# Cross attention and feed-forward on one core: scale sums on ScalarE, bias on the heads, one rope product, rounding by conversion

## What is computed

```python
x = x + xattn(layernorm(x), ctx, ctx, Wq, bq, Wk, bk, Wv, bv, Wo, bo)
x = x + ffn(layernorm(x), w_gate, w_up, w_down)

def xattn(Q, K, V, Wq, bq, Wk, bk, Wv, bv, Wo, bo):      # H = 16, HD = 32
    q, k = rope(heads(Q @ Wq.T + bq)), rope(heads(K @ Wk.T + bk))
    v = heads(V @ Wv.T + bv)
    scores = where(causal, q @ k.T / sqrt(HD), -inf)
    return merge(softmax(scores) @ v) @ Wo.T + bo

def ffn(x, w_gate, w_up, w_down):     # lpbq: blocks of 32, rounded to steps of max/7, clipped to -8..7
    up, gate = qdq(qdq(x) @ lpbq(w_up).T), qdq(qdq(x) @ lpbq(w_gate).T)
    gate = qdq(gate * u16(sigmoid(gate)))
    return qdq(gate * up) @ lpbq(w_down).T
```

## Time and profile before

| | us |
|---|---|
| three timed runs: median (lowest, highest) | 1614.03 (1614.02, 1615.21) |
| the profiled execution: its time | 1613.66 |
| the profiled execution: its span | 1611.8 |
| TensorE busy | 1394.6 (87%) |
| VectorE busy | 1235.3 (77%) |
| ScalarE busy | 921.6 (57%) |
| GpSimd busy | 321.2 (20%) |

### The profile page before, as it was taken

The page is one execution under the profiler, slowest core; times in us unless marked ns, Lnnn a source line. Parts: engine busy times, 40 slices in busy tenths (PEclk is TensorE's granted clock), DMA queues, the critical chain, the costliest instruction groups (busy, mean ns, idle before and its releaser), DMA issues.

```text
span 1611.8 us, 24568 instructions
## 1 busy us (share of the span) xinstructions
PE 1394.6 (87%) x9268; PEld 788.2 (49%) x9268; DVE 1235.3 (77%) x2002; ACT 921.6 (57%) x1994; POOL 321.2 (20%) x326
## 2 busy tenths in 40 slices
PE   4679999999999999967999998999999103999999
PEld 3356666666666667643444444444444001444444
DVE  6657788889898988756888776788899889745641
ACT  2557777777777778755222222899844796321210
POOL 1124444444444444540111110000000000000000
PEclk9879999999999999988999999999999555999999
DMA  5101111111122121111233333577655894534532
GB/s 202 66 8 64 50 65 62 60 65 63 65 79 80 66 80 53 41 42 64 97 113 118 118 112 119 184 250 250 228 183 176 320 356 166 203 137 158 193 132 79
DMA packets 84982, 200.05 MB, mean 124 GB/s; under 512 B 8065, under 2 KB 8065, under 8 KB 84865
## 3 DMA queue, kind: packets, MB, share of 16 engines
q1 hardware_dynamic: 84864, 198.48, 35.2%
HBM read 128.19 MB, written 70.25 MB: 123 GB/s over the span
## 4 chain that ended last, share of the span: by engine, by line
PE 47%; issue 6%; DVE 2%; ACT 0%; POOLq 0%; POOL 0%
PE ffn_banks L1092 31%; PE ffn_banks L1110 16%; PE ffn_banks L1068 1%; DVE ffn_wide L1251 0%; DVE ffn_peaks L1258 0%; DVE ffn_rises L1256 0%; DVE ffn_wide L1250 0%; DVE qg L1351 0%; ACT ffn_rest L1150 0%; ACT ffn_ring L1141 0%; DVE ffn_wide L1385 0%; ACT qg L1150 0%; PE ffn_banks L1098 0%; DVE ffn_wide L1398 0%; DVE ffn_wide L1392 0%
## 5 line engine op out<-in xcount | busy, mean ns | idle before, releaser
L1092 PE MATMUL ffn_banks<-ffn_wide,ffn_rest 128*128 128x512 f16 x2304 | 506.2, 381 | 10.4 <-DVE ffn_wide L1251 6.1
L1092 PEld LDWEIGHTS ffn_banks<-ffn_wide,ffn_rest 128*128 128x128 f16 x2304 | 226.2, 98 | 280.9 <-issue 17.1
L1110 PE MATMUL ffn_banks<-ffn_rest,ffn_wide 128*128 128x512 f16 x1152 | 251.4, 382 | 103.3 <-DVE ffn_wide L1392 103.3
L609 ACT ACTIVATE qg<-score_banks,neg_max 128x128 f32<-128x128 f32 (+1 forms) x512 | 208.0, 446 | 52.8 <-DVE neg_max L516 52.8
L1110 PEld LDWEIGHTS ffn_banks<-ffn_rest,ffn_wide 128*128 128x128 f16 x1152 | 113.3, 98 | 241.4 <-issue 107.2
L1150 ACT ACTIVATE ffn_rest<-ffn_banks,ffn_row_back 128x1024 f32<-128x1024 f32 x72 | 79.7, 1107 | 155.6 <-PE ffn_banks L1092 145.9
L1222 ACT ACTIVATE ffn_u_steps<-ffn_ring,ffn_scales 128x1024 int16<-128x1024 f32 x48 | 55.1, 1149 | 154.2 <-DMA ffn_ring<-ups_dram 135.4
L413 POOL TENSOR_TENSOR qg<-qg,per_sum 128x512 f32<-128x512 f32 x64 | 70.1, 1095 | 306.5 <-DVE per_sum L520 306.5
L415 POOL TENSOR_TENSOR qg<-qg,per_sum 128x1024 f32<-128x1024 f32 x64 | 121.1, 1892 | 0.0
L609 ACT ACTIVATION_READ_ACCUMULATOR qg<-score_banks,neg_max 128x1 f32 x512 | 119.1, 233 | 0.0
L657 PE MATMUL ring_banks<-xt,attn_hi 128*128 128x256 f16 x512 | 89.8, 277 | 10.2 <-DVE ct L501 6.2
(11 more groups left out here) (178 smaller groups left out, 2718.9 us busy)
## 6 DMA issues: line engine op xcount, KB each, us to landing
ffn_ring<-ups_dram SPq DMA_DIRECT2D x60, 512.0 KB, 4.1
ups_dram<-ffn_rest SPq DMA_DIRECT2D x48, 512.0 KB, 3.0
ffn_wide<-ups_dram SPq DMA_DIRECT2D x33, 512.0 KB, 9.4
gates_dram<-ffn_rest SPq DMA_DIRECT2D x24, 512.0 KB, 2.7
ffn_ring<-gates_dram SPq DMA_DIRECT2D x24, 512.0 KB, 4.6
...
```

Of the source, the lines that this page charges most:

```text
L609: last = act.activation(prob[:, s % 2, h, lo:hi], score_banks[:, h, lo:hi], ACT.Exp, bias=neg_max[:, s % 2, part, h:h + 1], accum_out=row_ ...
L1092: last = pe.matmul(banks[:, pair_of(s), half, :], w[:, m % 2, wp, c, :], xq[:, xp, n, c, :], start=(k == 0), stop=(k == 3 * DC - 1))
L1110: last = pe.matmul(down_banks[:, g % 2, t, :], oq[:, g % 2, op, m, t * P:(t + 1) * P], w_down[:, wp, wk, c], start=(start and k == 0), sto ...
```

## The change

The scales no longer come from the largest size but from the sum of sizes, times a factor: ScalarE reads a tensor in pieces of 1024 elements with `Abs` and an accumulated output (`sum_sizes`), TensorE adds the pieces over the partitions with ones as weights into one column each, and VectorE takes the power of two. `scanc`, `scanw`, `scand` and `join` leave VectorE. Batch 1 gets a context scale of its own, so `MX` counts one more. The bias of V is scaled once (`bv_scaled`) and added where the heads are evicted (`othi`, `otlo`); `bv`, `BIAS` and `bias` are gone. The tables of cosines and sines are one tensor, and rope's two products one instruction of 1024 elements. The quotient of a weight is written to int16, which rounds it, and then clipped. The weights of the attention are loaded in halves, the second context tile after the second tile of x.

```diff
-JOINS = ((0, 3), (3, 2)) + tuple((4 + n, 1) for n in range(1, 9))
+JOINS = ((0, 3), (3, 2)) + tuple((5 + n, 1) for n in range(9))
+SUM_SCALE = 2.0 ** -17
+HEADROOM = 2.0 ** 4
...
+ACT_AFTER = {(i, "exps", 0): [("sumc", 0, 2 * k), ("sumc", 0, 2 * k + 1)] for i, k in LATE_SETS}
 for k in range(DOWN_SCANS):
-    DVE_AFTER[DOWN_SCAN + k, "recip", 1] = [("scand", k, 0)]
+    ACT_AFTER[DOWN_SCAN + k, "exps", 2] = [("sumd", k, 0)]
+DVE_AFTER = {(i, "max", 2): [("scale", 2 + k, 0)] for i, k in LATE_SETS}
...
             load_c(0)
-            load_c(1)
             load_attn(MQ)
             load_attn(MK)
...
             load_x(1)
+            load_c(1)
             load_c(2)
...
                     if i == 0:
-                        await_free(pool, "BIAS", 0, 0)
+                        pool.wait_ge(bias_in, 16)
...
-                    dve.tensor_reduce(top[:, lo:lo + n], banks[:, b, 0:n * P].rearrange("p (k q) -> p k q", k=n), AX.X,
-                                      ALU.max).then_inc(emptied[b], 1)
+                    cols = slice(lo, lo + n)
+                    dve.tensor_scalar(top[:, cols], banks[:, b, 0:n], HEADROOM, TINY, ALU.mult, ALU.max).then_inc(emptied[b], 1)
...
                     if lo == V_COL:
+                        dve.wait_ge(consts_in, 16 * 3)
+                        link(dve.tensor_scalar(bv_scaled[:, :], bv[:, :], inv[:, V_COL:V_COL + 1], None, ALU.mult))
...
-                    link(dve.tensor_tensor(by_sin[:, :, :], raw[:, s % 2], sin[:, :, :], ALU.mult))
-                    dve.tensor_tensor(by_cos[:, :, :], raw[:, s % 2], cos[:, :, :], ALU.mult).then_inc(raw_used, 1)
+                    if DVE_COUNT["rope", g, i] > 1:
+                        dve.wait_ge(rotated, DVE_COUNT["rope", g, i] - 1)
+                    dve.tensor_tensor(turns[:, :, :, :], raw[:, s % 2].unsqueeze(1).to_broadcast([P, 2, 2, SEQ]),
+                                      tables[:, :, :, :], ALU.mult).then_inc(raw_used, 1)
+                    dve.wait_ge(raw_used, DVE_COUNT["rope", g, i])
...
-                    dve.tensor_tensor(ot[:, i % 2, 1, g, :], banks[:, b, 0:SEQ], ot[:, i % 2, 0, g, :],
-                                      ALU.subtract).then_inc(emptied[b], 1)
+                    dve.scalar_tensor_tensor(out=ot[:, i % 2, 1, g, :], in0=banks[:, b, 0:SEQ], scalar=bv_scaled[:, g:g + 1],
+                                             in1=ot[:, i % 2, 0, g, :], op0=ALU.add, op1=ALU.subtract).then_inc(emptied[b], 1)
...
                 if name == "wqc":
-                    link(dve.tensor_scalar(w_deq[:, :], w_deq[:, :], MAGIC, MAGIC + WMAX, ALU.add, ALU.min))
                     link(dve.tensor_scalar(step[:, :], step[:, :], row_inv[:, :], None, ALU.mult))
-                    dve.tensor_scalar(w_deq[:, :], w_deq[:, :], MAGIC - WMAX - 1.0, MAGIC, ALU.max,
-                                      ALU.subtract).then_inc(w_rounded, 1)
+                    dve.tensor_scalar(w_deq[:, :], w_q[:, :], -WMAX - 1.0, WMAX, ALU.max, ALU.min).then_inc(w_rounded, 1)
...
+            def sum_sizes(src, at):
+                if SUM_TURN[at] > 1:
+                    act.wait_ge(summed, SUM_TURN[at] - 1)
+                act.activation(unread[:, :], src, ACT.Abs, scale=SUM_SCALE, accum_out=sums[:, at:at + 1]).then_inc(summed, 1)
...
-                        last = pe.matmul(banks[:, b, k * P:(k + 1) * P], ones[:, :], spread[:, k, :], start=True, stop=True)
...
+                        parts_of = sums_of_column(lo + k)
+                        for j, at in enumerate(parts_of):
+                            pe.wait_ge(summed, SUM_TURN[at])
+                            last = pe.matmul(banks[:, b, k:k + 1], ones[:, :], sums[:, at:at + 1], start=(j == 0),
+                                             stop=(j == len(parts_of) - 1))
```

185 lines of the change are left out of this document (80 added, 105 removed).

## The result

The changed kernel takes 1631.49 us (median, 1628.23 to 1632.97), the kernel before 1614.03: a ratio of 1.0104, with a 95% interval of 1.0087 to 1.0121. It is 17.5 us slower; I had forecast 2 us more, 1616.1 us, and a range that ends at 1626. The profiled execution took 1628.23 us with a span of 1626.4, 14.6 us above that of before.

A forecast was written before the change was run, and what follows sets the result against it. TensorE was taken as the bound, its attention waits going straight into the time. Terms -9.9 + 14.4 + 6.6 - 8.0 - 1.1 = +2.0 us on the profiled 1613.66, plus 0.37 to the median: 1616.1 us, range 1602 to 1626.

The forecast's parts named there:

- The start: Before the attention loop: earlier scales and no bias matmuls bring the scores of group 3 to 76.9 us: -9.9 us.
- The late sums: Six odd iterations: two context sums on ScalarE free x_in later, delaying scores of group 2 by 2.4 us each: +14.4 us.
- TensorE's clock: Odd iterations: the clock drops after the 3.45 us wait in two of three cases, 1.65 us each: +6.6 us.
- VectorE behind the maxima of group 1: Attention iterations: L560 goes, the reciprocal comes earlier, and TensorE's wait for GpSimd at the transposes shrinks: -8.0 us.
- Rival B: Scores of group 2, six odd iterations: clock falls every time and stays down longer, +8.4 us, 1624.5 us; chance 0.20.
- rival E: VectorE's edits: the single product waits for its own write, the int16 clamp runs slow (0.69 us); 1621 us; chance 0.08.
- Down sums: Six single sums of 1.13 us behind the exponentials of group 2, covered by the group's TensorE work: 0.
- the scans and joins: VectorE loses six down-weight scans and the diagonal products; TensorE's two waits for x2 go: -1.1 us.
- Rope elsewhere, bias on the heads: 64 ropes shrink by 0.07 us in VectorE's slack; bias in the head evictions adds no instruction: 0.

The follow-up runs named there:

- bn_before: Kernel before, with the statistics of the next x tile behind the maxima of group 1 in VectorE's list instead of ahead of them: 1627.58 us.
- ropes_fill: Changed kernel with overwritten matmuls in the waits before the scores of group 2, and VectorE's old rope products and three-operation rounding put back: 1624.90 us.
- fill2_after: Changed kernel with overwritten matmuls in the waits before the scores of group 2, iterations 2 to 13 (12 where a scale set follows, 6 elsewhere): 1614.81 us.
- the shortened loop: Changed kernel with x statistics behind group 1's maxima, gate weights' clamp behind the reciprocal, GpSimd's group 1 normalising ahead of its dequantisation: 1597.56 us.
- chain_sumd: Changed kernel with shortened chain and late context sums apart, plus the six down-weight sums moved behind the exponentials of group 3 instead of group 2: 1588.46 us.

## Why the prediction was wrong, step by step

**The start**, -9.9. Right. First projections at 21.86 us (I wrote 22.5; 25.97 in the earlier trace rows), scores of group 3 at 74.89 (76.9; 86.77 in the earlier trace rows), scores of iteration 1 at 98.15 (100.6; before 110.47): -12.3. Over all kernels here the start of the first maxima of iteration 1 is at 110.2 to 112.7 us without the change and 99.7 to 102.4 with it, so that some 10 us are the change's and 2 are chance.

**The late sums**, 6 x 2.4. Right in mechanism and near in size: 2.27 us of delay, 3.49 us of wait, a single sum of 1.04 to 1.14 us and an accumulator read of 0.18 to 0.28. One thing was wrong in it, that nothing else waits less for the later scores: the 0.80 us for VectorE at the transposes of group 0 went. That the scores of group 2 are bound to the load of x, and to nothing TensorE does, was confirmed by bn_before.

**TensorE's clock**, +6.6. This is the step that failed, as a term that was mis-sized and in one part missing. I took a drop "in two cases of three" in the odd iterations, each worth 1.65 us, and none in the even ones, because five of six waits of 2 us had passed before. Measured: twelve falls in twelve iterations, five of them at waits that had not changed, four of double length. The price of one fall was near: filled against unfilled, profile by profile, an iteration with 3.4 us of low clock lost 1.0 to 1.8 us and one with 6.8 lost 2.3 to 2.9 (iteration 4 left out, whose wait was another). The number of falls was wrong: twelve, not four. Filling iterations 2 to 13 brings 16.7 us back, 10.1 more than the term.

Not all of the 16.7 us is the clock's alone, because the falls hide VectorE's gain: with VectorE's old steps the same filling brings back 6.5 us (1631.39 - 1624.90). The two terms together are safer to read. Clock and VectorE's new steps cost 1631.49 - 1624.90 = +6.6 us, and I had +6.6 - 8.0 = -1.4 for them. That is 8.0 of the 15.4 us that I missed. Iteration 1, which that filling did not reach, took 5.2 us more than before (I had 2.4 + 1.1 for it) and came down to 39.7 us once it was filled and its sums moved. The end of the attention part took 3.0 us more, with equal waits. The start was 2.4 us better than my term. Some 5 us of the miss no run here assigns. Rival B, the clock falls each time, came true in kind, but I had priced it for six places only. Five waits that passed were no five separate trials: they came at regular intervals, in the kernel with six extra matmuls three of them turned together, and in the one with twelve that of iteration 4 turned with nothing changed ahead of it.

**VectorE behind the maxima of group 1**, -8.0. The place was right and the size was near, with the clock up: 10.1 us by ropes_fill against fill2_after, some 7 without the fall that is in it. In iteration 8 the reciprocal starts 5.34 us behind the second maxima, in iteration 8 of the kernel before 6.67. That L560 vanishes was not the point, though. Its successor in VectorE's list takes the stall:

```profile
412.42 2.36 POOL L407 TENSOR_TENSOR x_res<-x_res,bias_row 128x1024 f32<-128x1024 f32 x1 [2.79 <-DMA x_res<-in_x]
...
413.60 1.20 DVE L539 TENSOR_SCALAR step<-step,row_inv 128x16 f32<-128x16 f32 x1
414.84 0.43 DVE L540 TENSOR_SCALAR w_deq<-w_q 128x512 f32<-128x512 int16 x1
```

Sixteen elements take 1.20 us, to the end of GpSimd's operation (414.78). The clamp from int16 costs 0.43 us, so rival E fell; the product took 1.22 us. The gain did not reach the time, because I added it to the price of the falls as if the two were independent. They are not: a fall behind the scores slows the 4 us of work in front of the transposes, and this hides just the wait that VectorE's steps shorten. In the kernel before with one delay, the wait of 1.1 us at the transposes is missing in iterations 6, 8 and 10, which had the falls. Where the clock falls, nothing of the gain is left (the new steps were 0.1 us slower).

**Down sums**, 0, "covered", and the scans and joins, -1.1. TensorE's waits for x2 are gone from the list of 112 to 600 us. The sums cost nothing that shows in the waits of the changed kernel as it is. In the shortened loop they cost: chain_sumd gained 6.1 us by moving them.

**Rope elsewhere, bias on the heads**, 0. No run isolates them; nothing in the traces waits for either. The feed-forward half is unchanged, as said.
